# Local attention: the inverse norms of queries and keys as a clipped power on GpSimd, in place of a logarithm, an exponential and a Newton step on ScalarE and VectorE

## The reference

```python
def l2norm(t):
    return t / jnp.clip(jnp.linalg.norm(t, axis=-1, keepdims=True), 1e-12)

def _layer(x, wqkv, qs, ksc, wo, lg, lb, w1, b1, w2, b2):
    h = shift_token(x)
    q, k, v = jnp.split(h @ wqkv, 3, axis=-1)          # 8 heads of 64 channels each
    q, k, v = (to_heads(q), to_heads(k), to_heads(v))
    q = l2norm(q) * qs
    k = l2norm(k) * ksc
    q, k = rotary_xpos(q, k)
    o = local_attention(q, k, v)                       # windows of 64, the own one and the one before
    x = x + o.transpose(0, 2, 1, 3).reshape(b, n, INNER) @ wo
    h = layernorm(shift_token(x)) @ w1 + b1
    a, g = jnp.split(h, 2, axis=-1)
    return x + (a * gelu(g)) @ w2 + b2
```

## Time and profile before

| | |
|---|---|
| median of three timed runs | 1976.98 us (1975.87 to 1977.96) |
| profiled execution, first to last instruction | 1971.5 us |
| mean granted TensorE clock of that execution | 0.986 of full speed |
| PE, DVE, ACT, POOL busy | 97, 82, 75, 46% of the span |
| tiles of local attention | 4 x 32 |
| instructions on POOL | 549 |

### The profile page before, as it was taken

The page is one execution under the profiler, slowest core; times in us unless marked ns, Lnnn a source line. Parts: engine busy times, 40 slices in busy tenths (PEclk is TensorE's granted clock), DMA queues, the critical chain, the costliest instruction groups (busy, mean ns, idle before and its releaser), DMA issues. The chain is left out here.

```text
span 1971.5 us, 52907 instructions
## 1 busy us (share of the span) xinstructions
PE 1906.8 (97%) x18490; PEld 1129.9 (57%) x18490; DVE 1623.9 (82%) x5453; ACT 1483.3 (75%) x4089; POOL 916.0 (46%) x549
## 2 busy tenths in 40 slices
PE   7999999999999989999999999899999999999998
PEld 4777763577775343434434367437777646777743
DVE  6999964899994579999999769779999548999844
ACT  5999993799997253777777754469999837999962
POOL 2787860578781040000000046337878406787700
PEclk9999999999999997999999999999999999999999
DMA  6121220112120040111111000002212201121301
GB/s 188 43 48 43 48 60 6 35 43 49 42 66 23 6 152 28 41 42 42 42 42 43 19 5 2 2 21 47 49 43 47 55 6 42 42 49 42 70 12 43
DMA packets 76106, 85.08 MB, mean 43 GB/s; under 512 B 17139, under 2 KB 50499, under 8 KB 75715
## 3 DMA queue, kind: packets, MB, share of 16 engines
q1 hardware_dynamic: 75647, 81.68, 16.3%
q10 hardware_dynamic: 196, 0.02, 0.0%
HBM read 21.14 MB, written 8.39 MB: 15 GB/s over the span
## 5 line engine op out<-in xcount | busy, mean ns | idle before, releaser
L304 ACT ACTIVATE probs<-probs,negmax 128x128 f32<-128x128 f32 x1024 | 399.8, 396 | 23.2 <-DVE negmax L377 22.1
L2083 ACT ACTIVATE gprobs<-ps_global 128x1024 f32<-128x1024 f32 (+3 forms) x384 | 291.4, 810 | 124.3 <-PE ps_global L1548 101.2
L259 POOL TENSOR_TENSOR rot<-rot 128x1024 f32<-128x1024 f32 x128 | 302.5, 2363 | 145.6 <-DVE rot L347 145.6
L265 POOL TENSOR_TENSOR qk<-rot,cnorm 128x1024 f32<-128x1024 f32 x128 | 243.8, 1905 | 120.1 <-POOL rot L259 89.5
L272 POOL TENSOR_TENSOR probs<-probs,iden 128x1024 f32<-128x1024 f32 x128 | 242.9, 1898 | 120.0 <-DVE iden L385 120.0
L1778 DVE TENSOR_REDUCE maxes<-ps_global 128x1 f32<-128x512 f32 (+2 forms) x384 | 222.0, 637 | 10.2 <-PE ps_global L1511 6.5
L377 DVE CUSTOM_DVE_ANT_0 probs<-ps_attn,masks 128x128 f32<-128x128 f32 x1024 | 226.2, 285 | 0.0
L1506 PE MATMUL ps_global<-kq 48*128 48x512 bf16 (+3 forms) x768 | 196.7, 345 | 7.2 <-DVE maxes L1778 1.8
L304 ACT ACTIVATION_READ_ACCUMULATOR probs<-probs,negmax 128x1 f32 x1024 | 197.0, 192 | 0.0
L345 DVE TENSOR_TENSOR rot<-ps_attn,rotary 128x512 f32<-128x512 f32 x256 | 174.8, 683 | 1.8 <-PE ps_attn L171 1.6
L239 PEld LDWEIGHTS ps_attn<-probsT,v_first 128*64 128x64 f32 x2048 | 118.1, 136 | 98.1 <-ACT probsT L325 94.3
(11 more groups left out here) (212 smaller groups left out, 4585.0 us busy)
## 6 DMA issues: line engine op xcount, KB each, us to landing
v_first<-v_second SPq DMA_DIRECT2D x256, 128.0 KB, 2.3
hs<-z_a SPq DMA_DIRECT2D x256, 32.0 KB, 1.9
ln<-z_b SPq DMA_DIRECT2D x56, 128.0 KB, 2.4
kq<-split_scratch SPq DMA_DIRECT2D x64, 96.0 KB
kq<-split_scratch SPq DMA_DIRECT2D x64, 64.0 KB
split_scratch<-parts SPq DMA_DIRECT2D x8, 384.0 KB, 4.1
split_scratch<-gprobs SPq DMA_DIRECT2D x6, 384.0 KB, 3.9
x_tok<-in_x_dram SPq DMA_DIRECT2D x4, 512.0 KB, 6.4
```

The costliest lines, as they stand in the source:

```text
L259: nc.gpsimd.tensor_tensor(a, a, b, ALU.add).then_inc(C["rot_sum"], 1)
L265: nc.gpsimd.tensor_tensor(qk[:, k % 2, :].rearrange("p (h d) -> p h d", d=DH), rot_a[:, k % 2, :, :], cnorm[:, k % 2, :].unsqueeze(2).to_b ...
L304: last = nc.scalar.activation(probs[:, k % 2, slot, :], probs[:, k % 2, slot, :], ACT.Exp, scale=-1.0, bias=negmax[:, k % 2, slot:slot + 1 ...
L2083: nc.scalar.activation(probs[:, step % RING, 2 * p:2 * p + 2, 0:w], ps[:, S0 + 2 * p:S0 + 2 * p + 2, 0:w], ACT.Exp).then_inc(C["p2_exp"], 1)
```

## The change

The inverse norm of a tile becomes two instructions on POOL, in front of the scaling that uses it: the sums of squares are clipped from below at 1e-24 (so that the root's inverse stays at or below 1e12), and a tensor-tensor power takes them to -0.5, the exponent being a constant tile of 128x16. `act_norm`, `dve_clip_norm`, four tiles and their semaphores go. `dve_ssq`, which writes one of two halves in turn, now waits for the clip of two tiles earlier, where it waited for the logarithm. On POOL the new steps stand behind the sum of the tile after and ahead of the scale. The norms of the global attention are left as they are.

```diff
@@ constants
+NORM_LEAST = 1e-24
@@ tiles
-        lnorm = sb("lnorm", [P, 2, 2 * HEADS])
-        inorm = sb("inorm", [P, 2, 2 * HEADS])
-        newton = sb("newton", [P, 2, 2 * HEADS])
         cnorm = sb("cnorm", [P, 2, 2 * HEADS])
+        minus_half = sb("minus_half", [P, 2 * HEADS])
@@ GpSimd
+        def gp_inverse_norm(gp, wait, i, k):
+            wait("ssq_done", i, k)
+            n = cnorm[:, k % 2, :]
+            nc.gpsimd.tensor_scalar(n, ssq[:, k % 2, :], NORM_LEAST, None, ALU.max).then_inc(C["norm_clipped"], 1)
+            wait("norm_clipped", i, k)
+            nc.gpsimd.tensor_tensor(n, n, minus_half[:, :], ALU.pow).then_inc(C["norm_ready"], 1)
+
         def gp_rotary_scale(gp, wait, i, k):
+            gp_inverse_norm(gp, wait, i, k)
             wait("rot_sum", i, k)
             wait("norm_ready", i, k)
             wait("k_turned", i, k, 2)
@@ ScalarE
-        def act_norm(act, wait, i, k):
-            wait("ssq_done", i, k)
-            nc.scalar.activation(lnorm[:, k % 2, :], ssq[:, k % 2, :], ACT.Ln, bias=K["norm_bias"][:, 0:1],
-                                 scale=NORM_SCALE).then_inc(C["norm_log"], 1)
-            wait("norm_log", i, k)
-            nc.scalar.activation(inorm[:, k % 2, :], lnorm[:, k % 2, :], ACT.Exp, bias=K["norm_shift"][:, 0:1],
-                                 scale=-0.5).then_inc(C["norm_inv"], 1)
@@ VectorE
         def dve_ssq(dve, wait, i, k):
             wait("k_squared", i, k)
-            wait("norm_log", i, k, 2)
+            wait("norm_clipped", i, k, 2)
             nc.vector.reduce_sum(ssq[:, k % 2, :], sq[:, :].rearrange("p (h d) -> p h d", d=DH), AX_X
                                  ).then_inc(C["ssq_done"], 1)
-        def dve_clip_norm(dve, wait, i, k):
-
-            r, n = inorm[:, k % 2, :], newton[:, k % 2, :]
-            wait("norm_inv", i, k)
-            nc.vector.tensor_tensor(n, r, r, ALU.mult).then_inc(C["newton"], 1)
-            wait("newton", i, k, 0, 2, 1)
-            nc.vector.scalar_tensor_tensor(out=n, in0=n, scalar=-0.5, in1=ssq[:, k % 2, :], op0=ALU.mult, op1=ALU.mult
-                                           ).then_inc(C["newton"], 1)
-            wait("newton", i, k, 0, 2)
-            nc.vector.scalar_tensor_tensor(out=n, in0=n, scalar=1.5, in1=r, op0=ALU.add, op1=ALU.mult
-                                           ).then_inc(C["newton_done"], 1)
-            wait("newton_done", i, k)
-            wait("qk_ready", i, k, 2)
-            nc.vector.tensor_scalar(cnorm[:, k % 2, :], n, NORM_MOST, None, ALU.min).then_inc(C["norm_ready"], 1)
@@ start of GpSimd's list
+            nc.gpsimd.memset(minus_half[:, :], -0.5)
             nc.gpsimd.memset(v_first[0:64, 0, :], 0.0).then_inc(C["pass_set"], 1)
+            gp.wait_ge(C["pass_set"], C.after("pass_set", 2))
@@ bodies, seams and ends: every call of act_norm and of dve_clip_norm goes, as in
             def body(i, k):
                 if ahead(i, k, 1):
                     act_exp(act, wait, *tile_of(i, k + 1), range(2, 4))
-                if ahead(i, k, 3):
-                    act_norm(act, wait, *tile_of(i, k + 3))
                 if ahead(i, k, 0):
                     act_probsT(act, wait, i, k)
```

More of the change, by code:

```diff
@@ L92 @@
 ATTENTION_SEMS = (
-    "k_done", "q_done", "v_done", "k_rotated", "q_rotated", "q_squared", "k_squared", "ssq_done", "norm_log", "norm_inv", "newton",
-    "newton_done", "norm_ready", "rot_sum", "qk_ready", "q_turned", "k_turned", "qT_ready", "kT_ready", "scores_done", "max_done",
+    "k_done", "q_done", "v_done", "k_rotated", "q_rotated", "q_squared", "k_squared", "ssq_done", "norm_clipped", "norm_ready", "rot_sum", "qk_ready", "q_turned", "k_turned", "qT_ready", "kT_ready", "scores_done", "max_done",
     "exp_done", "inv_done", "probs_ready", "p5_turned", "p6_turned", "p5_read", "p6_read", "v_ready", "av_done", "heads_ready",
@@ L844, in attention_end @@
                 act_exp(act, wait, *t(layer, 29), range(2, 4))
-                act_norm(act, wait, *t(layer, 31))
                 act_probsT(act, wait, *t(layer, 28))
@@ L922, in _ @@
             act_ln_log(act, -1, 5)
-            act_norm(act, wait, *t(0, 0))
             act_ln_inverse(act, -1, 5)
@@ L931, in _ @@
             act_ln_inverse(act, -1, 7)
-            act_norm(act, wait, *t(0, 1))
             act_values(act, wait, *t(0, 0))
@@ L940, in _ @@
             act_kT(act, wait, *t(0, 1))
-            act_norm(act, wait, *t(0, 2))
             act_exp(act, wait, *t(0, 0), range(0, 3))
@@ L964, in _ @@
             act.preload_act_table_set(EXP_LN_SET)
-            act_norm(act, wait, *t(1, 0))
-            act_norm(act, wait, *t(1, 1))
             act_values(act, wait, *t(1, 0))
@@ L971, in _ @@
             act_square_k(act, wait, *t(1, 2))
-            act_norm(act, wait, *t(1, 2))
             act_qT(act, wait, *t(1, 1))
@@ L1001, in body @@
                     dve_probsT(dve, wait, i, k)
-                if ahead(i, k, 3):
-                    dve_clip_norm(dve, wait, *tile_of(i, k + 3))
                 if ahead(i, k, 4):
@@ L1016, in attention_end @@
                 dve_probsT(dve, wait, *t(layer, 28))
-                dve_clip_norm(dve, wait, *t(layer, 31))
                 dve_inv(dve, wait, *t(layer, 29))
@@ L1060, in _ @@
             dve_rotate(dve, wait, 1, *t(0, 1))
-            dve_clip_norm(dve, wait, *t(0, 0))
             dve_ln_scale(dve, -1, 5)
@@ L1066, in _ @@
             dve_ln_scale(dve, -1, 7)
-            dve_clip_norm(dve, wait, *t(0, 1))
             dve_rotate(dve, wait, 1, *t(0, 2))
@@ L1071, in _ @@
             dve_max(dve, wait, *t(0, 0))
-            dve_clip_norm(dve, wait, *t(0, 2))
             dve_rotate(dve, wait, 1, *t(0, 3))
@@ L1106, in _ @@
             hides(0, 22, 23)
-            dve_clip_norm(dve, wait, *t(1, 0))
-            dve_clip_norm(dve, wait, *t(1, 1))
             hides(0, 23, 24)
@@ L1114, in _ @@
             dve_max(dve, wait, *t(1, 0))
-            dve_clip_norm(dve, wait, *t(1, 2))
             dve_rotate(dve, wait, 1, *t(1, 3))
@@ L1156, in _ @@
                 first.sync_decay(sp)
-    once = {name: DEPTH * TILES for name in ATTENTION_SEMS if name not in ("newton", "max_done")}
-    C.close(newton=2 * DEPTH * TILES, max_done=HEADS * DEPTH * TILES, pass_set=2, ln_low=DEPTH, ln_high=DEPTH,
+    once = {name: DEPTH * TILES for name in ATTENTION_SEMS if name != "max_done"}
+    C.close(max_done=HEADS * DEPTH * TILES, pass_set=2, ln_low=DEPTH, ln_high=DEPTH,
             **{f"ln_in{m}": DEPTH * (32 if m == 3 else 64) for m in range(4)},
```

## The result

The changed kernel takes 2218.42 us (median, 2215.20 to 2221.03) against 1976.65 for the kernel before in the same comparison. The ratio is 1.1224, 95% interval 1.1208 to 1.1239: 12% slower. The forecast was 1971.6 with a range to 2090; rival A, by its formula, has the right mechanism with too low a price.

A forecast was written before the change was run, and what follows sets the result against it. GpSimd and VectorE, waiting on each other, set a 7.58 us round, with PE's 7.53 just beneath. 4 x 28 x (7.582 - 7.534) = 5.4 us off 1976.98 gave 1971.6 us, range 1964 to 2090.

The forecast's parts named there:

- rival A: The power is dear and GpSimd's queue sets every round, from a power of 1.10 us on; chance 0.41.
- The ring through the held Newton step: VectorE and GpSimd waiting on each other through sum, Newton's remainder, rotations, reciprocal and normalise set the old round, 7.58 us.
- PE's 7.53: PE's own round in the main loop with nobody in its way, 0.05 us under the round of 7.58.
- The hold: VectorE's small Newton step with two SBUF inputs (L360) waits until GpSimd's large sum ends; its group's mean is 443 ns.
- the price of the power: GpSimd's power over 128x16, between sum and scale: 0.87 us, as 50 steps of 14 ns over 170 ns.
- the upper end: Dearest power on GpSimd: some 50 to 60 elementary steps at 35 ns each, 2.3 us, giving 2116 us.
- 6.48 + X: GpSimd's new round in us: sum, maximum, wake-ups, scale and normalise make 6.48, and X is the power's duration.
- The point from which PE's 7.53 is passed: The power's duration up to which GpSimd's new round stays under PE's own: 1.05 us.
- four rounds' 7: Rounds beyond the 28 in each of four stretches, one more at each end, within the 116 that pay for a dear power.
- Worth of the rest: Gain when the power is cheap and PE's rate sets the main loop's round: 5.4 us, with 0 at the seam.
- The offset: Time outside the first and last instruction, by which the median 1976.98 exceeds the profiled span 1971.5: 5.5 us, unchanged by the edit.
- DVE and ACT less busy by 125 and 78 us: Sign of a right forecast: VectorE about 125 us less busy without its small steps, ScalarE 78 without Ln and Exp.

The follow-up runs named there:

- the product: The changed kernel with the power replaced by a product, norms not computed: 1966.21 us against 1975.49, ratio 0.9953.
- the idle additions: The changed kernel with a product for the power, plus idle VectorE steps (reduce, then two-input or one-input addition) during GpSimd's sum: 1968.43 and 1969.16 us.
- the probe: The changed kernel with a product for the power, plus powers of several shapes on GpSimd before the first tile: each 0.42 us + 0.155 us per column.
- With 8 columns: The changed kernel with the power over only the first 8 of the 16 columns: 2047.39 us, ratio 1.0361.

## Why the prediction was wrong, point by point

- **The bound before: right.** The ring through the held Newton step at 7.58, with PE's 7.53 under it, was confirmed from three sides: without the Newton step, with the step on POOL, and with the product the round stops at 7.53 each time. The hold was the right reading of L360's 443 ns, as the idle additions show.
- **The step that failed is the price of the power.** The prediction put 0.87 us, as 50 elementary steps of 14 ns over 0.17, and took 2.3 as the upper end. It is 2.93, that is 0.155 us a column. With 50 steps each would cost 3.1 ns a column; the prediction had 0.87. That figure was the slope of a cast, and nothing but a guess said that a step of a power costs as little; that such steps stay in registers, no run shows. The upper end was no bound either: its 35 ns a step came from rows of an addition, but the count was the same guess. The Trainium skill ("GPSIMD Engine Reference", Performance pitfalls for Q7 kernels) has 4 cycles an element for a dependent chain, which gave 2.7 us with the same 50 steps. By the 1.2 GHz of the same page (Specifications) the probe's slope, 155 ns, would be 186 cycles, or 46 such steps; that is an estimate near the 50, and no run shows that the code is such a chain or how many steps it has.
- **Rival A's formula: right.** It said 6.48 + X; measured are 6.51 + X at three values of X, the 0.03 being a maximum of 0.25 in place of 0.18, less 0.04 by which the gaps between the instructions fell short of those put for them. The point from which PE's 7.53 is passed, 1.05, is 1.02. PE waits for POOL before the transposes of q and k, as rival A said, but not before those of the probabilities.
- **Rival A's sum was short even so.** With 2.93 its formula gives (9.41 - 7.58) x 116 = 212 us on 1977, about 2189, and 2218 was measured. Between the two profiled spans it is short by 32: 15 us are in the 112 rounds, nearly all of it the long ones at the lower clock, and 17 before, between and behind them, which cost 24 where the prediction counted four rounds' 7. Of the 24 some 4.4 are the three long rounds at the lower clock near the layers' ends (8.81 to 8.87 for 7.36); no run takes the rest apart.
- **Worth of the rest: low by 4 us.** With the product 9.3 us came off the median, not 5.4, and 8.0 between the two profiled spans (1971.5 and 1963.5). Counted between PE's probability transposes, the four times 28 rounds give 5.75 of these, about as worked out. Tile 28's round is 8.10 in place of 8.65, four times, or 2.2, and 1.3 came off between the passes, terms that the prediction left out. The run's start and end gave 1.3 back. What the medians have beyond the spans is a difference between executions.
- **The offset.** The prediction put 5.5 us outside the first and last instruction. For the changed kernel it is 1.8 (2217.81 and 2216.0 for one execution). The rest was a difference between executions. The sum was one of differences, so nothing hung on it.
- **DVE and ACT less busy by 125 and 78 us: wrong, 93 and 37.** The durations, added up one by one, fell by 123 and 74, about as said. Busy time counts the stretches in which neighbours overlap only once, and so fell by less.

## What to carry to other kernels

Before work moves to an engine with half its time free, write down that engine's ring in one round. POOL was busy for 46% of the run, but in a round of 7.58 it had 1.41 us of idle time, so a maximum and a power of more than about one microsecond were bound to show there. The price of an operation that no row shows is not bounded by a guessed count of steps: where it decides between faster and slower, a row of it in idle time, as in the probe, is the first thing to measure. And a small step on VectorE beside a large one on GpSimd may cost the large one's remainder: here a reduce went free, and a two-input instruction and a tensor-scalar on SBUF, all of 16 columns in fp32, did not.

## What the runs showed of the hardware

- A GpSimd power costs 0.42 us + 0.155 us per column, for 16 partitions as for 128 (2.90 us for 128x16, 2.89 for 64x16, and for 16x16 2.89 or, beside a busy VectorE, 3.15); a product of 128x16 0.22.
- VectorE's tensor-tensor with two SBUF inputs, and its tensor-scalar with one, each of 16 columns, wait for the end of a running GpSimd addition of 128x1024 and end 0.03 to 0.04 us behind it, in 112 of 112 rounds each. The reduce of 16 columns takes 0.16 there.
- With PE idle for 1.8 us in a round of 9.44, the lower clock (1.2 GHz) was granted in 17 of 112 rounds, and each of these was about 0.9 us longer. With 8 columns, where PE is idle for 0.57 in a round of 8.18, it was granted in none of the 112, and the mean clock stayed at 0.986, the value of the kernel before.
